# Experts: the eight transfers that pad the token buffer move from tiles 9 to 12 to tiles 7 to 10 of the load queue

## The reference

```python
probs = softmax(xf @ router_w.T)
topk_probs, topk_idx = top_k(probs, 2)
topk_probs = topk_probs / sum(topk_probs)
combine = zeros((N, E)).at[arange(N)[:, None], topk_idx].add(topk_probs)
h = gelu_new(einsum('nc,ech->neh', xf, w_fc) + b_fc)
out = einsum('neh,ehc->nec', h, w_proj) + b_proj
y = einsum('nec,ne->nc', out, combine)
x = x + tanh(g_ffn[0]) * y
```

## Time and profile before

| what | value |
|---|---|
| median of 3 timed runs | 819.77 us (819.17 to 822.52) |
| span of the profiled execution | 881.7 us |
| TensorE busy in the profiled execution | 708.1 us (80%) |
| VectorE busy | 710.4 us (81%) |
| ScalarE busy | 566.2 us (64%) |
| GpSimd busy | 585.0 us (66%) |
| mean DMA rate | 145 GB/s |

### The profile page before, as it was taken

The page is one execution under the profiler, slowest core; times in us unless marked ns, Lnnn a source line. Parts: engine busy times, 40 slices in busy tenths (PEclk is TensorE's granted clock), DMA queues, the critical chain, the costliest instruction groups (busy, mean ns, idle before and its releaser), DMA issues. The chain is left out here.

```text
span 881.7 us, 19709 instructions
## 1 busy us (share of the span) xinstructions
PE 708.1 (80%) x6550; PEld 550.0 (62%) x6550; DVE 710.4 (81%) x1855; ACT 566.2 (64%) x1172; POOL 585.0 (66%) x570
## 2 busy tenths in 40 slices
PE   6998999999998998699369978988984789476435
PEld 3776777777776776577247767877872567233134
DVE  4999988888888998489166757767876899889988
ACT  4666566767676664576046656666766787488756
POOL 4675588888887788677746544656555898188810
PEclk9999899999999999899769989999996999755759
DMA  8414532323232222757348778878775933000005
GB/s 241 137 38 141 109 129 66 134 68 131 96 104 80 91 97 103 256 169 227 115 144 266 225 205 252 253 249 256 232 235 174 353 98 108 15 1 0 1 24 169
DMA packets 95430, 127.69 MB, mean 145 GB/s; under 512 B 20529, under 2 KB 65153, under 8 KB 94305
## 3 DMA queue, kind: packets, MB, share of 16 engines
q1 hardware_dynamic: 85760, 108.00, 40.0%
q0 software_dynamic: 8672, 17.99, 5.9%
q10 hardware_dynamic: 896, 0.43, 0.2%
HBM read 82.76 MB, written 43.53 MB: 143 GB/s over the span
## 5 line engine op out<-in xcount | busy, mean ns | idle before, releaser
L590 POOL DMA_INDIRECT m_results<-a_probs,e_to x142 | 146.9, 1035 | 106.6 <-ACT a_probs L827 59.4
L614 POOL TENSOR_TENSOR a_probs<-a_probs,a_top 128x1024 f32<-128x1024 f32 x64 | 122.0, 1906 | 57.0 <-DVE a_top L1682 56.0
L805 ACT ACTIVATE room<-a_ps_s,e_bias 128x512 f32<-128x512 f32 (+1 forms) x160 | 102.0, 652 | 85.8 <-PE a_ps_s L1111 54.8
L571 POOL DMA_INDIRECT m_tokens_to<-r_rows,r_place x128 | 133.9, 1046 | 32.3 <-issue 32.1
L1702 DVE CAST e_hp<-room 128x512 fp32r<-128x512 f32 (+1 forms) x160 | 67.8, 424 | 78.7 <-remote 32.2
L722 ACT ACTIVATE a_probs_t<-a_ps_pt 128x512 f32<-128x512 f32 x128 | 69.8, 592 | 84.5 <-PE a_ps_pt L1011 84.1
L1704 DVE TENSOR_TENSOR e_hp<-room,e_hp 128x512 fp32r<-128x512 f32 (+1 forms) x160 | 102.8, 643 | 5.5
L1634 DVE TENSOR_TENSOR a_probs<-a_ps_s,a_mask 128x1024 f32<-128x1024 f32 x64 | 77.9, 1217 | 13.4 <-PE a_ps_s L892 7.5
L995 PEld LDWEIGHTS a_ps_o<-a_vals,a_probs_t 128*64 128x64 f32 x2048 | 69.3, 140 | 30.0 <-issue 29.0
L995 PE MATMUL a_ps_o<-a_vals,a_probs_t 128*64 128x18 f32 x2048 | 77.2, 214 | 8.2 <-issue 7.0
L1682 DVE TENSOR_REDUCE a_top<-a_probs 128x16 f32<-128x1024 f32 x64 | 77.2, 1206 | 0.1
(11 more groups left out here) (422 smaller groups left out, 1901.6 us busy)
## 6 DMA issues: line engine op xcount, KB each, us to landing
e_weights<-m_weights_to SPq DMA_DIRECT2D x80, 512.0 KB
m_weights_to<-r_parts SPq DMA_DIRECT2D x8, 1024.0 KB
room<-m_tokens_to SPq DMA_DIRECT2D x31, 264.0 KB
c_two<-m_results SPq DMA_DIRECT2D x3, 1536.0 KB, 10.8
a_ctx_in<-in_ctx_dram SPq DMA_DIRECT2D x17, 256.0 KB, 2.8
m_keys_t<-n_keys SPq DMA_DIRECT2D x16, 256.0 KB
m_values<-n_values SPq DMA_DIRECT2D x16, 256.0 KB
out_dram<-x_all SPq DMA_DIRECT2D x15, 256.0 KB, 2.4
```

What stands on the lines that cost most here:

```text
L571: pool.indirect_dma_start(tokens_to, bass.IndirectOffsetOnAxis(ap=place[:, k, q:q + 1], axis=0), rows[:, c % RING, q % CT, k, :], None).th ...
L590: pool.indirect_dma_start(results, bass.IndirectOffsetOnAxis(ap=to[:, v, r:r + 1], axis=0), y[:, v, r], None).then_inc(returned[v], 16)
L614: pool.tensor_tensor(probs[:, j], probs[:, j], top[:, j].unsqueeze(2).broadcast_to([P, HEADS, SEQ]), ALU.subtract).then_inc(shifted, 1)
L805: act.activation(h[:, c, at], ps_h[c][:, at], ACT.Gelu_apprx_tanh, bias=bias[:, n % ROWS, c:c + 1]).then_inc(h_sb, 1)
```

## The change

The point from which the pairs of paddings go out becomes a name, `PADDINGS_AT`, and its value is 7 where it was `EARLY - 4` = 9. The wait for `ends_ready` moves along with the first pair. The loop now also has an upper bound, as tiles follow the last pair. The pair of experts 0 and 1 goes out at n = 7, the last pair at n = 10. The wait for `padded` ahead of `load_rows(13)` stays.

```diff
+PADDINGS_AT = EARLY - 6
@@ in the program of SP
         for n in range(SETS, EARLY):
             if n + ROWS_AHEAD < EARLY:
                 load_rows(n + ROWS_AHEAD)
-            if n == EARLY - 4:
+            if n == PADDINGS_AT:
                 sp.wait_ge(ends_ready, 1)
-            if n >= EARLY - 4:
-                for e in range((n - EARLY + 4) * 2, (n - EARLY + 4) * 2 + 2):
+            if PADDINGS_AT <= n < PADDINGS_AT + EXPERTS // 2:
+                for e in range((n - PADDINGS_AT) * 2, (n - PADDINGS_AT) * 2 + 2):
                     padding_of(sp, e)
             if n + 1 < EARLY:
                 load_up(n + 1)
             load_down(n)
```

## The result

| kernel | median | runs | ratio to before (95%) |
|---|---|---|---|
| before | 819.65 us | 15 (814.45 to 822.52) | |
| after | 815.33 us | 15 (810.63 to 818.62) | 0.9948 (0.9928 to 0.9968) |
| after, a second time | 814.62 us | 12 (811.51 to 820.09) | 0.9955 (0.9927 to 0.9983) |

The change makes the kernel 0.5% faster, 4.3 us at the medians. The prediction was 819.5 us with no change as the likeliest, and its range began at 817.0. It was wrong.

What follows compares the result with a forecast made beforehand. TensorE was taken to set the expert stage's pace; terms 0 + 0 + 0 + 0 - 0.3 = -0.3 us took 819.8 to 819.5 us (profiled 881.7 to 881.4), with a range of 817.0 to 822.5.

Steps and rivals of the forecast that it cites:

- The disturbed stretch: Profile from 418.6 to 451.3, 32.7 us for one tile; taken for a profiling disturbance, the timed run reckoned with 6.4 us.
- The load of tile 13's rows: Its wait for all eight pads goes; bounds 0 and -1.0 us, -0.3 us taken.
- rival B: The wait at tile 13 was a true stall in timed runs; at most 3.4 us faster, 816.4; chance 0.07.
- Those of tile 12 wait for TensorE itself, not for the pads: Tile 12's weights, at 477.30, were held by TensorE; nothing gained where tiles 11 and 12 lose their pairs.
- SP's rounds: With a pair 7.3 us against TensorE's 6.4; four such rounds let SP lag 3.6 us at most by tile 10, absorbed.
- The wait for the ends: SP meets it at tile 7, its preceding load's issue ending 1.34 us after the ends are written; cost 0.
- the pads at tiles 7 and 8: A pair each delays weight loads by 2.4 us; slack 3.5 us at tile 7, 0.9 less at tile 8; cost 0.
- Rival A: Weights late behind the pads at tiles 7 and 8, with a slower clock; 6.8 us slower, 826.6; chance 0.09.
- SP's first pad: Sign in the profile after: the first pad about 1.1 us behind the row load of tile 9.
- tile 13's rows followed tile 12's weights: Sign in the profile after: the row load about 1.1 us behind tile 12's second weights, not 2.18.
- Rival C: The disturbed stretch belongs to transfers and moves with them; -3.9 to +3.9 us, 815.9 to 823.7; chance 0.06, half either side.

Runs made afterwards that it cites:

- the undisturbed profile: The kernel before, unchanged, profiled a second time; 820.56 us, ratio 1.0018 (0.9994 to 1.0042).
- the rows held less: The changed kernel, SP holding the load of tile 13's rows until the last product but one group of tile 10; 816.55 us, ratio 0.9972.
- registers only: The changed kernel with five register loads ahead of each of tiles 11 and 12 and no transfers behind them; 817.75 us, timed once.
- the kernel one tile later: The changed kernel with the pairs ahead of tiles 8 to 11, one tile later; 815.29 us, ratio 0.9965.
- the unwaited extra transfers: The changed kernel with two extra pad-sized transfers ahead of each of tiles 11 and 12, not waited for at tile 13; 817.71 us, ratio 1.0008.
- the kernels with held rows: The changed kernel, tile 13's row load held until tile 10's last product, or the last but one group; 818.02 and 816.55 us.

## Why the prediction was wrong

**The disturbed stretch: right as read, wrong in its use.** It was taken for a disturbance of one profiled execution, and it was: no other profile has it. But the prediction then trusted margins from rows behind it. In the earlier trace rows the stretches from 451.3 and 466.8 are 9.1 and 10.3 us long; in them TensorE was slow, and SP had time to catch up. The last pair went out 5.3 us ahead of tile 12's transposes there (471.79 and 477.05), in place of 0.69, and tile 12's second weights left 0.25 us behind them, and not 1.97. The stretch from 451.3 in that trace, at a clock of 0.70:

```profile
451.30:460.40 9.10, 9.03 (x33) 7.14 (x32) 8.89 (x36) 5.60 (x12) 5.64 (x5) 0.70 0.73 215
```

**The step that failed: "The load of tile 13's rows".** It was rightly named as the one place where the pads can be on the path. Its size was off: bounds of 0 and -1.0 us and a value of -0.3 stood where the undisturbed profile has -4.1. Three things make up the difference. First, the load came 6.48 us behind tile 12's transposes, not 2.43 as in the first trace (479.48 and 477.05), and TensorE stood still for 2.24 us. Secondly, "at most 1.04 us was wait for the pads" was true of that trace; undisturbed it is 3.1. Thirdly, the clock's part, 1.7 us, stood in rival B but not in the bounds. The landing of the rows was not the trouble: the "somewhat under 4.7 us" for 264 KB was 2.96 us from issue to use.

**"Those of tile 12 wait for TensorE itself, not for the pads": wrong.** In the undisturbed profile SP was still issuing pads when TensorE was done with tile 9, and the weights left 1.7 us later than in after. The prediction weighed SP's rounds, 7.3 us with a pair against TensorE's 6.4, but for the new order only, and its 7.3 us was read between 451.70 and 458.97, where TensorE was slow as well. Undisturbed, the round from tile 12's rows to the next pair takes 6.47 us (419.51 to 425.98), and SP is in step at tile 12's rows in both orders. What was never counted is what SP still has to issue from there until tile 12's second weights are due, some 12.4 us: three pairs in the old order, 7.8 us with their register work, and one in the new. With the one SP ends up 4.0 us early.

**What held.** The wait for the ends cost nothing, and the pads at tiles 7 and 8 cost TensorE nothing: from tile 3 to tile 12 it takes 59.6 us both before and after. (It takes 60.2 to 62.0 us in four of the other profiles, by a longer gap that lies ahead of the first pad; see the last section.) Rival A has no sign anywhere. SP's first pad was 1.1 us behind its rows, and tile 13's rows followed tile 12's weights by 1.48 us (1.1 was forecast). Rival C falls with the long stretches, which go along with neither place of the pads.

**Rival B was the case**, at a chance of 0.07. Its price, 1.0 + 2.4 = 3.4 us, is near the 2.4 + 1.7 = 4.1 measured, with the gap too small and the clock too dear. Its reason, a stall in the timed runs, was right; why the stall comes, SP's lateness, is in no rival. The argument held against it, "TensorE's row at 484.12 has no idle in front", was an argument from the disturbed trace. The 4.64 us of lead there against up to 4.7 of landing should have raised the chance: the margin in after, undisturbed, is 5.32 us from issue to use.

## What to carry to other kernels

If a profiled span is much longer than the timed runs, don't read a margin from the rows behind the disturbed stretch: a slowed engine hands slack to all that feed it. Work out the queue that feeds it instead, against the undisturbed pace, for the order before as well as for the one after. Begin at the last point at which the issuing engine is in step with the others, here tile 12's rows, and add up what it has to issue from there until the load that matters is due. Two rare pairs less in that stretch, some 5 us, decided whether a transfer with a completion to be waited for went out before or behind that point. Put rare work ahead of a point at which the issuing engine has to wait anyway.

## What the runs showed that was not expected

The clock doesn't answer to every gap, and the gap's length doesn't settle it. At tile 13, behind gaps of 1.03, 1.07, 1.54 and 1.88 us, TensorE kept a granted clock of 1.00; behind 2.24 and 2.26 us it fell to half, the lower of its two levels (1.2 GHz), and tile 14 took 8.0 us where it takes 6.3. The window from 442.8 to 446.2 us of the second profile of before:

```profile
442.80:446.20 3.40, 3.40 (x10) 2.64 (x9) 1.20 (x3) 2.09 (x6) 2.79 (x3) 0.50 1.01 304
```

That looks like a length between 1.88 and 2.24 us that decides, which the expectation for the rows held less took up. Another gap in the same profiles speaks against it. Between tiles 4 and 5, ahead of the first pad, TensorE waits for VectorE's `r_chosen` in all of them, 1.0 to 1.1 us in most and 1.7 to 1.9 us in four. Here are that gap and the 6.3 us behind it, in the kernel with pairs at 7, 8, 11 and 12 and then in the one with registers only:

```profile
387.99 0.19 PE L984 MATMUL a_ps_o<-r_chosen,r_before 128*128 128x64 bf16 x1 [1.74 <-DVE r_chosen L1287]
388.00:394.30 6.30, 6.30 (x26) 5.27 (x27) 6.02 (x18) 2.66 (x7) 5.42 (x5) 0.73 0.79 236
```

```profile
385.68 0.19 PE L987 MATMUL a_ps_o<-r_chosen,r_before 128*128 128x64 bf16 x1 [1.76 <-DVE r_chosen L1290]
385.70:392.00 6.30, 6.30 (x33) 5.29 (x34) 6.13 (x18) 3.74 (x10) 5.42 (x5) 1.00 0.78 240
```

The clock fell behind 1.74 us (and behind 1.91 us in the kernel one tile later), and not behind 1.76. So gaps under 2 us are not safe, and what else decides stays open. It also means that the 1.7 us of before need not be lost in every execution.

Rows that leave later can need less time: from issue to use 2.96 us in before, against 3.91 us with the unwaited extra transfers ahead. But it is 3.71 us with registers only, where no pad is near and tile 12's second weights, 512 KB, went out 1.4 us ahead, and 2.65 and 2.61 us in the kernels with held rows, where they went out over 5 us ahead. So holding a load until what is ahead has landed costs less than the wait's length, by some 1 us here.
